# Quantised feed-forward layer: transposes by DMA, and mixing and residual as 64x64 products

## The reference

```python
x  # (64, 64, 512); conditions: 64 numbers; weights (200, 64, 64); weight (512, 512); bias (512)
w = weights[conditions]
y = jnp.einsum('bct,bcd->bdt', x, w)
...
xb = x.reshape(*shape[:-1], shape[-1] // BLOCK, BLOCK)          # BLOCK = 32
amax = jnp.max(jnp.abs(xb), axis=-1, keepdims=True)
exp = jnp.floor(jnp.log2(jnp.maximum(amax, jnp.finfo(x.dtype).tiny))) - FP4_EMAX
scale = jnp.where(amax > 0, jnp.exp2(exp), jnp.ones_like(amax))
q = jnp.clip(xb / scale, -FP4_MAX, FP4_MAX)
aq = jnp.abs(q)
lsb = jnp.where(aq < 2.0, 0.5, jnp.where(aq < 4.0, 1.0, 2.0))
qr = jnp.round(q / lsb) * lsb
return (qr * scale).reshape(shape)
...
out = jnp.einsum('mk,nk->mn', a, w) + bias
x = x + out
```

## Time and profile before

| | us |
|---|---|
| median of 3 runs | 111.22 (110.67 to 111.39) |
| the profiled execution's own time | 110.9 |
| its span, from the first to the last instruction | 109.2 |
| VectorE busy | 92.5 (85%) |
| TensorE busy | 80.3 (74%) |
| ScalarE busy | 79.0 (72%) |
| GpSimd busy | 34.3 (31%) |
| bytes moved by DMA | 23.70 MB, mean 217 GB/s |

### The profile page before, as it was taken

The page is one execution under the profiler, slowest core; times in us unless marked ns, Lnnn a source line. Parts: engine busy times, 40 slices in busy tenths (PEclk is TensorE's granted clock), DMA queues, the critical chain, the costliest instruction groups (busy, mean ns, idle before and its releaser), DMA issues.

```text
span 109.2 us, 1704 instructions
## 1 busy us (share of the span) xinstructions
PE 80.3 (74%) x440; PEld 39.9 (37%) x440; DVE 92.5 (85%) x145; ACT 79.0 (72%) x113; POOL 34.3 (31%) x55
## 2 busy tenths in 40 slices
PE   5994900299140999799969969997996994389960
PEld 4952200363010834263443435335353341324420
DVE  5245999999509986999999999999999999999970
ACT  3433298006993559999999999999999999873300
POOL 4393999846754475130030003003001100300000
PEclk9999998558985589999999999999999999999999
DMA  1996989979597510339389596938948777694995
GB/s 38 401 372 136 301 304 394 332 214 357 186 295 260 192 35 22 119 76 199 101 304 180 108 362 130 180 141 285 196 113 327 144 144 285 171 207 134 350 385 203
DMA packets 13850, 23.70 MB, mean 217 GB/s; under 512 B 3846, under 2 KB 4370, under 8 KB 13842
## 3 DMA queue, kind: packets, MB, share of 16 engines
q1 hardware_dynamic: 11506, 17.83, 46.7%
q0 software_dynamic: 2048, 5.26, 23.7%
q10 hardware_dynamic: 288, 0.52, 1.3%
HBM read 10.49 MB, written 8.39 MB: 173 GB/s over the span
## 4 chain that ended last, share of the span: by engine, by line
DVE 59%; PE 16%; ACT 9%; issue 6%; DMA 5%; SPq 2%; DVEq 0%; ACTq 0%
DVE n_int L512 11%; DVE top L524 10%; DVE a L533 10%; DVE low L499 7%; PE y_ps L252 6%; DMA w_sb<-in_L_ffn_weight_dram 5%; DVE inv L504 4%; PE o_ps L265 3%; DVE n_int L517 3%; PE o_ps L276 3%; ACT zone L372 3%; DVE m L460 3%; DVE amax L477 2%; DVE m L466 2%; DVE s L483 2%
## 5 line engine op out<-in xcount | busy, mean ns | idle before, releaser
L252 PE MATMUL y_ps<-x_sb,mix 128*128 128x512 f32 x64 | 32.6, 639 | 4.1 <-DMA mix<-in_L_cond_weights_dram 4.1
L276 PE MATMUL o_ps<-wT,aT 128*128 128x512 bf16 x120 | 27.5, 380 | 0.0
L356 ACT ACTIVATE z<-y_ps 128x512 bf16<-128x512 bf16 x32 | 19.1, 621 | 8.4 <-PE y_ps L252 7.8
L265 PE MATMUL o_ps<-ident,a 128*128 128x128 bf16 x128 | 10.2, 242 | 17.6 <-DVE a L533 17.6
L157 POOL DMA_DIRECT2D mix<-in_L_cond_weights_dram x32 | 17.4, 546 | 13.2 <-issue 11.9
L372 ACT ACTIVATE zone<-inv 128x2048 int16<-128x2048 int16 (+1 forms) x10 | 17.5, 1755 | 3.8 <-DVE inv L504 3.7
L512 DVE TENSOR_TENSOR n_int<-y_sb,inv 128x1024 int16<-128x1024 f32 x16 | 19.0, 1222 | 0.8
L235 POOL DMA_DIRECT2D x_sb<-o_sb x6 | 5.3, 882 | 44.8 <-ACT o_sb L380 44.8
L364 ACT COPY y_sb<-y_ps 128x512 f32<-128x512 f32 x32 | 18.5, 607 | 0.0
L252 PEld LDWEIGHTS y_ps<-x_sb,mix 128*128 128x128 f32 x64 | 12.4, 207 | 15.8 <-issue 15.0
L265 PEld LDWEIGHTS o_ps<-ident,a 128*128 128x128 bf16 x128 | 8.6, 109 | 23.9 <-DVE a L533 15.5
(11 more groups left out here) (38 smaller groups left out, 55.6 us busy)
## 6 DMA issues: line engine op xcount, KB each, us to landing
x_sb<-in_x_dram SPq DMA_DIRECT2D x7, 1024.0 KB, 6.5
x_sb<-o_sb POOLq DMA_DIRECT2D x6, 768.0 KB, 5.8
out_dram<-x_sb SPq DMA_DIRECT2D x6, 768.0 KB, 3.5
out_dram<-x_sb SPq DMA_DIRECT2D x14, 256.0 KB, 3.0
x_sb<-in_x_dram SPq DMA_DIRECT2D x2, 512.0 KB, 4.9
w_sb<-in_L_ffn_weight_dram ACTq DMA_DIRECT2D x2, 256.0 KB, 3.4
w_sb<-in_L_ffn_weight_dram SPq DMA_DIRECT2D x2, 256.0 KB, 5.7
mix<-in_L_cond_weights_dram POOLq DMA_DIRECT2D x32, 16.0 KB, 3.5
```

The lines of the kernel that those rows point to most:

```text
L252: nc.tensor.matmul(y_ps[:, t, :], mix[:, (step - 1) * GROUP + t, :], x_tiles(step, t), start=True, stop=True).then_inc(y_ready, 1)
L265: last = nc.tensor.transpose(t_bank(step, t)[:, c * P:(c + 1) * P], a2[:, t, c * P:(c + 1) * P], ident[:, :])
L276: last = nc.tensor.matmul(o_bank(step, t), aT[:, t, c, :], wT[:, c, :], start=False, stop=(c == KC - 1))
L356: nc.scalar.activation(blocked(z[:, step % 2, t, :]), permuted_high(y_ps[:, t, :]), ACT.Abs, scale=ZONE_GAIN).then_inc(z_ready, 1)
```

## The change

**Products.** `mix` holds only the 64x64 matrices, without zeros. A float32 product is now 64 rows deep and 64 columns wide, in one quarter of the array: rows from half r of the partitions, results to half g (`QUARTERS` gives the order of the four). `mix_pair` makes two banks of `y_ps` from four such products; `residual_pair` puts 4 times x into two banks of `o_ps` in the same way, with a 64x64 identity times `GAIN` = 4, ahead of bias (which is also multiplied by 4) and of the sixteen weight products. The weight is no longer scaled by 0.25; instead the factor 1/4 is in the copy from `o_ps` to `x_sb`. No engine adds x any more, and `o_sb`, the accumulating DMA and the adds of VectorE are gone. Since the two batch items of one tile now stand in other places, x is loaded in two DMAs of 64 partitions for each step.

**Transposes.** `a2` of steps 1 to 7 and of the weight is transposed by DMA, issued by SyncE (`turn`: two DMAs of two tiles each; one DMA for the weight), straight into `aT` (now with two buffers) and `wT`. Step 8 is still turned on TensorE, into banks of `y_ps`, and copied by ScalarE. `rescale` waits for the DMA that read `a2` of the step before (`aT_in`).

**Order.** The weight tiles of SyncE's queue are loaded ahead of x, half of the first x by GpSimd; the bias is split by VectorE with four operations ahead of the first tree; mixing of steps 1 and 2 no longer has the weight's transposes between. On SyncE the stores of step s - 1 stand ahead of the transposes of step s.

```diff
+        QUARTERS = ((0, 0), (1, 1), (0, 1), (1, 0))
+        HALVES = (slice(0, C), slice(C, P))
...
+            def turn(step, half):
+
+                sp.dma_start_transpose(aT[:, step % 2, 2 * half:2 * half + 2, :, :].rearrange("p t c m -> p (t c) m"),
+                                       a2[:, 2 * half:2 * half + 2, :].rearrange("p t k -> p (t k)")
+                                       ).then_inc(aT_in[half], 16)
...
+            for step in range(1, LAST):
+                if step > 1:
+                    for t in (0, 2):
+                        sp.wait_ge(copied_out, tiles_done(step - 1, t + 1))
+                        store(step - 1, t, 2)
+                sp.wait_ge(a2_done, step + 1)
+                if step > 2:
+                    sp.wait_ge(o_ready, tiles_done(step - 2, GROUP - 1))
+                turn(step, 0)
+                turn(step, 1)
+                if step + 5 <= STEPS:
+                    load_step(step + 5)
...
-                nc.tensor.matmul(y_ps[:, t, :], mix[:, (step - 1) * GROUP + t, :], x_tiles(step, t),
-                                 start=True, stop=True).then_inc(y_ready, 1)
...
+                for i, (r, g) in enumerate(QUARTERS):
+                    n = 2 * q + g
+                    last = nc.tensor.matmul(y_ps[HALVES[g], 2 * q + r, :],
+                                            mix[HALVES[r], (step - 1) * GROUP + n, :], x_tiles(step, n)[HALVES[r], :],
+                                            start=True, stop=True)
+                    if i >= 2:
+                        last.then_inc(y_ready, 1)
+
+            def residual_pair(step, q):
+                for r, g in QUARTERS:
+                    nc.tensor.matmul(o_bank(step, 2 * q + r, HALVES[g]), ident_4[HALVES[r], :],
+                                     x_tiles(step, 2 * q + g)[HALVES[r], :], start=True, stop=False)
...
+            def start_group(step):
+                for q in range(2):
+                    if step > 1:
+
+                        pe.wait_ge(copied_out, tiles_done(step - 1, 2 * q + 1))
+                    residual_pair(step, q)
                 for t in range(GROUP):
                     bias_tile(step, t)
...
-                nc.scalar.copy(o_sb[:, step % 2, t - ADDED:t - ADDED + n, :], o_ps[:, t:t + n, :]).then_inc(copied_out, n)
...
+                nc.scalar.mul(x_tiles(step, t, n).rearrange("p (n t) -> p n t", n=n), o_ps[:, t:t + n, :], 1 / GAIN
+                              ).then_inc(copied_out, n)
```

More of the change, by code:

```diff
@@ L18 @@
 GROUP = 4
-ADDED = 1
+GAIN = 4.0
 WARMUPS = 18
@@ L344, in _ @@
+            for t in range(GROUP):
+                ffn_tile(LAST, t)
         @block.scalar
@@ L527, in rescale @@
             def rescale(step, done, rounded, t0=0, n=GROUP):
-                if step > 0 and t0 == 0:
-                    dve.wait_ge(t_ready, GROUP * step)
+                if step == 1:
+                    dve.wait_ge(wT_in, 16)
+                elif step > 1:
+                    for half in range(t0 // 2, (t0 + n) // 2):
+                        dve.wait_ge(aT_in[half], 16 * (step - 1))
                 dve.wait_ge(n_done, rounded)
@@ L599, in _ @@
                 rescale(LAST, LAST + 1 + half, 2 * LAST + 1 + half, 2 * half, 2)
[L600 to L602 removed]
+            copy_out_last(1)
+            copy_out_last(3)
 _INS = ["x", "itok_B_1_198", "L0_cond_weights", "L0_ffn_weight", "L0_ffn_bias"]
```

354 lines of the change are left out of this document (158 added, 196 removed).

## The result

The changed kernel takes 116.14 us (median of 4 runs, 114.47 to 119.18) against 111.06 us for the kernel before in the same job. Two of its five executions, the profiled one among them (time 117.3, span 115.7 us), were in a slower state, and the ratio of 1.034 (95% interval 1.028 to 1.041) goes by the other three alone. The change made the kernel 3.4% slower; 6.2% faster was forecast. The three had spans of 112.8 to 113.5 us, so some 2 us of what follows belong to the profiled execution; the trace doesn't say in which stretch.

A forecast was written before the change was run, and what follows sets the result against it. VectorE held 59% of the chain of waits, with three engines nearly full. Terms -1.0 - 0.94 - 4.3 - 2.3 - 1.0 + 2.6 = -6.94 took the span from 109.2 to 102.3, time 104.3 us; range 100.5 to 118.

The forecast's parts named there:

- TensorE, 7.4 us a step: Middle steps: TensorE needs 8.44 - 1.07 - 3.44 + 3.44 = 7.4 us, with quarter products overlapping at 0.22 us each.
- Rival 1: Mixing and residual products: two passes go in order, 0.43 us a quarter product, 10.8 us a step, 115.8 us; chance 0.22.
- Rival 4: Mixing and residual products: quarters don't overlap at all, a step of 17.7 us, about 160 us; chance 0.03.
- VectorE, 8.69 a step, and step 1, 8.7: VectorE loses one 0.60 us add, leaving 8.69 a step; step 1's waits go, 13.01 to 8.7, -4.3 us.
- L, 7.2 us: Time from issue of first store to landing of second transpose, 7.2 us; the loop lasts L + 1.9, 9.1 us.
- rival 2: Transposes by DMA are dear: gain gone at L = 8.2, 127 us at 6.4 us a step; chance 0.17.
- Steps 3 to 7: 5 x (9.1 - 9.29) = -1.0: Five middle steps go from 9.29 us to the store-and-transpose loop's 9.1 us each, -1.0 us in all.
- The end: +2.6: After the last step: late transposes leave products, copies and stores to follow, 13.50 to 16.1 us, +2.6.
- Step 2: -2.3, if loads of x don't hold `turn(1)`; they are issued well before: Step 2 goes from 11.01 to 8.7 us, provided 2 MB of x ahead in the queue don't hold its transposes.
- Weight ahead of x: -1.0: Start: the last weight tile, loaded ahead of 1 MB of x, comes some 1.0 us earlier, -1.0.
- The -0.94 of GpSimd: Start: with bias work off GpSimd, `limit` of step 0 falls from 2.17 to 1.23 us, -0.94.
- rival 3: Steps and end: the transpose loop is hidden, VectorE binds, 100.7 us; chance 0.50 together with the main case.

The follow-up runs named there:

- run 6: Run 1 plus eight products by a zero weight ahead of each step's weight products, as filler for TensorE: 107.40 us, ratio 0.966.
- run 12: Run 1 with the load of step 5 moved behind the transposes of step 1: 106.06 us, ratio 0.957.
- run 1: Changed kernel with each step's transposes ahead of the stores of the step before on SyncE, nothing else: 105.74 us, ratio 0.941.
- run 2: Changed kernel plus eight products by a zero weight ahead of each step's weight products: 114.94 us, ratio 1.030.
- run 3: Changed kernel with upper halves of x loaded by GpSimd's queue, lower by SyncE's: 114.94 to 124.05 us in four runs, too scattered for a ratio.
- run 13: Changed kernel, transposes ahead of stores, a quarter of bytes by 64-partition DMAs, load of step s + 4 behind transposes of step s: 99.52 us, ratio 0.894.
- run 14: Run 1, all x loads by 64 partitions, with the load of step s + 4 behind the transposes of step s: 103.19 us, ratio 0.929.
- run 5: Changed kernel with transposes ahead of stores, x loaded over 128 partitions and output stored in 64-partition halves: 102.67 us, ratio 0.924.
- run 4: Changed kernel with x loaded over 128 partitions in one DMA and output stored by 64 partitions in two: 137.06 us, ratio 1.214.
- run 7: Kernel before with its x load of steps 2 to 8 cut in two DMAs of 64 partitions: 111.85 us, ratio 1.003.
- run 9: Run 5 with each output tile stored in one DMA over 128 partitions: 230.73 us, ratio 2.08.

## Why the prediction was wrong

The direction was wrong. What it said of the computing engines held. The steps that failed are on the DMA queue: step 2, where it put the wait for two megabytes of x at nothing (12.8 us, not 8.7), and the loop, whose rounds it took as even (steps 3 to 7 51.2 us, not 45.5, and the end 18.2, not 16.1). By its own steps:

- **TensorE, 7.4 us a step.** Right. Quarter products 0.24 each (0.22), and TensorE needs some 7.5: run 6 has 9.42 with 1.9 of filler. Rivals 1 (passes in order) and 4 (no overlap) are refuted by the 1.95 us of mixing. (Rival 1 would have decided from 0.32 us a product on, by the prediction's own numbers, and not from 0.36: (9.1 - 3.93)/16.)
- **VectorE, 8.69 a step, and step 1, 8.7.** Right: 8.75 where nothing waits.
- **L, 7.2 us.** Right where nothing disturbs the round: from the first store at 77.64 to `rescale` at 84.51 it is 6.9, and the round is 8.9, as L + 1.9 says. The split was off: the transposes are issued 2.2 us behind the first store, and a pair then takes 4.7 until `rescale` goes on (3.6 to landing is the median of single transposes of 256 KB). But L is 7.8, 8.8 and 10.9 in the rounds that begin at 55.28, 65.08 and 41.36. Over 8 us was the prediction's sign for rival 2 (dear transposes), so that rival came true in two rounds, though not by the price of a transpose: run 12 shows the same pair at 2.6 and 6.6 us of issue, by what stands ahead.
- **"Steps 3 to 7: 5 x (9.1 - 9.29) = -1.0".** The loop was the right mechanism, and run 1 shows it. Its size failed: the four rounds from the store at 55.28 to that at 96.27 average 10.2 us, and the steps sum to 51.2, not 45.5. The good rounds last 8.9 to 9.8, near the 9.1 forecast. The round of 12.6 has two things that the sum lacked: loads of x in the queue, which let the transposes land 2.0 us later, and products at the lower clock after the longer wait, 1.6 us. Of the two the late landing is enough: run 2 takes the slow products away and has rounds of 11.0 and 10.5 us all the same, while run 3 takes half of x out of the queue and has 9.4, 8.9, 8.9 and, with one group at 5.21, 10.5. What delays the transposes of run 2 at 77.40, 16 us behind its last load of x, stays open.
- **"The end: +2.6".** The same loop, mis-sized: +4.7. With the loop gone the end is 13.6 (run 1), so all of the +4.7 was the loop. In run 2, where the products of step 6 take 3.63 us and not 5.31, the end is 16.6, near the 16.1 forecast; the rest of the miss is those slow products.
- **"Step 2: -2.3, if loads of x don't hold `turn(1)`; they are issued well before".** Failed, and it is the step with the clearest error: 12.84 in place of 8.7. The loads of steps 4 and 5 were issued from 23.59 us, the transposes from 30.67, but the engines were not done: the last landed at 42.1. The two megabytes ahead of them are the cause (runs 12 to 14). The earlier trace rows was enough to see a wait: at worst 2 x 6.5 us behind 23.6 is 36.6, later than 30.7, and with 3.2 for the transposes 39.8, where `rescale` of step 2 is due at 38.2. It was not enough to see 4 us.
- **"Weight ahead of x: -1.0".** Failed: the last weight tile is used at 10.89, not at 7.6, and mixing waits 6.92 us for its rows of `mix`. Runs 1, 2, 6, 12 and 14 have the same start; there the tile is used at 8.4 to 9.7 and mixing waits 5.2 to 7.0 us. So the 1.0 is in none of six profiles, and this profile is the worst of them. Step 1 begins at 24.73 here and at 23.02 to 24.78 in those five, with 23.3 forecast: the 1.4 us missed at the start are no more than one execution differs from the next. With full loads the tile is used at 8.2 and step 1 begins at 21.9 (run 5). The -0.94 of GpSimd held (`top` of step 0 in 1.22, `a` in 1.23 us).

The misses against the forecast are 1.4 (start), 4.1 (step 2), 5.7 (steps 3 to 7) and 2.1 (end). With the queue put right (run 13) the time is 99.5, below the 100.7 of rival 3, the case in which the loop is hidden: the end costs nothing extra, and the start is 1.3 us shorter, with loads laid out otherwise.

The 34 us between runs 4 and 5 are the loop again: steps 3 to 7 sum to 69.4 against 46.0 us, and the end is 26.1 against 15.8. A round of run 4 is some 4.7 us longer than a good one, in all three of its parts. How much of that is the half stores' slowness and how much the clock that falls in the longer waits stays open. That the diagonal layout and not the pacing gives the 3.7 us between runs 14 and 13 is shown by those two; how that divides into loads and stores is not.

## What to carry to other kernels

A DMA that an engine waits for in every step is queued with everything else on its queue: write down what stands ahead of it, in waits and in bytes, and put it ahead of stores that nobody waits for. If its own result leads to those stores, their order closes a loop, and the loop's length is the step. Load no further ahead than needed: bytes in front of a short transfer are a wait (two megabytes cost step 2 some 4 us here), and moving one load moves the wait to the next step unless all are paced.

Look at the partitions and the outermost dimension of every DMA that a new layout brings, ahead of its bytes.

## What the runs showed of the hardware

- Loads over 64 partitions keep all engines busy at 217 to 221 GB/s where loads over 128 move 263 to 308 at a share of 0.78 to 0.97 (run 7 against the kernel before); loading the halves from two queues does not help (180 to 232, run 3).
- A store whose DRAM side has an outermost dimension of 2 uses two engines, 51 GB/s (run 9).
- Four 64x64 float32 products in the array's quarters, two passes each, run at once: eight in 1.95 us, where one after the other they would take 3.44 even at one pass's 0.43 each.
- A transpose by DMA of 256 KB lands 3.6 us after its issue (median of 14 in the changed kernel, 2.9 to 10.1); two of them hold up `rescale` for 4.7 us from the first issue in a good round. Their issue takes SyncE 2.6 us with one megabyte of loads ahead and 6.6 with two (run 12).
